# A GRU and an attention GRU on one core: a second copy of x on the state's quadrants, another order of the matmuls, halves for one product, and the second stage's sum on VectorE

## The reference, cut to what matters

```
xp = keys @ Wx + b_in                      # 64 -> 3*64, per step: xz, xr, xh
rec = h @ Wh + b_rec                       # rz, rr, rh
z = sigmoid(xz + rz);  r = sigmoid(xr + rr)
hh = relu(xh + r * rh)
h = z * h + (1 - z) * hh                   # 1024 steps, outputs kept
logit = sum_u(outs * (queries @ W_att.T)); attn = softmax over time
# second recurrence over outs, a = attn of the step
r = sigmoid(xr + h @ W_r);  c = relu(xc + r * (h @ W_c))
h = (1 - a) * h + a * c                    # 1024 steps, the last h is the output
```

## Time and profile before

| what | value |
|---|---|
| median of 3 runs | 4726.49 us |
| the profiled execution, its own time | 4727.85 us |
| its span (first to last instruction) | 4726.0 us |
| PE, PEld, DVE, ACT, POOL busy | 98%, 92%, 89%, 50%, 77% of the span |
| granted TensorE clock, mean share of full speed | 0.998 |
| DMA traffic over the span | 115 GB/s |

### The profile page before, as it was taken

One profiled execution on the slowest core, in us unless ns is written; L12 is line 12 of the kernel. 1 busy time (PEld: TensorE's weight loads), 2 busy tenths in 40 slices (PEclk: granted clock), 3 DMA queues, 4 the chain that ended last, 5 costly groups with the idle time before them and its releaser, 6 DMA issues.

```text
span 4726.0 us, 366111 instructions
## 1 busy us (share of the span) xinstructions
PE 4648.7 (98%) x131196; PEld 4341.8 (92%) x131196; DVE 4188.5 (89%) x28719; ACT 2353.4 (50%) x9363; POOL 3629.2 (77%) x8204
## 2 busy tenths in 40 slices
PE   8999999999999999999998999999999999999999
PEld 8999999999999999999997999999999999999998
DVE  8999999999999999999997888888888888888888
ACT  5555555555555555555553333333333333333333
POOL 6777777777777777777776888888888888888888
PEclk9999999999999999999999999999999999999999
DMA  3333333333333333333334554555555555555554
GB/s 103 107 107 114 110 107 113 110 107 111 113 107 111 113 107 108 115 108 107 115 116 119 124 122 118 124 123 119 122 124 119 121 124 120 120 124 120 119 124 108
DMA packets 169276, 544.15 MB, mean 115 GB/s; under 512 B 31644, under 2 KB 38060, under 8 KB 169260
## 3 DMA queue, kind: packets, MB, share of 16 engines
q1 hardware_dynamic: 169260, 543.93, 43.7%
HBM read 405.24 MB, written 138.56 MB: 115 GB/s over the span
## 4 chain that ended last, share of the span: by engine, by line
PE 98%; issue 1%; DMA 0%; DVE 0%; POOL 0%; SPq 0%; ACT 0%; POOLq 0%; ACTq 0%; DVEq 0%
PE r_bank_a L531 14%; PE r_bank_b L531 13%; PE c_bank_b L531 12%; PE c_bank_a L531 11%; PE logit_bank L583 6%; PE z_bank_a L537 6%; PE r_bank_a L537 5%; PE z_bank_b L537 5%; PE z_bank_a L531 5%; PE r_bank_b L537 5%; PE z_bank_b L531 4%; PE c_bank_b L537 3%; PE c_bank_a L537 3%; PE c_bank_a L543 1%; PE c_bank_b L543 1%
## 5 line engine op out<-in xcount | busy, mean ns | idle before, releaser
L295 POOL TENSOR_TENSOR kept<-z_gate,h 128x128 f32<-128x128 f32 x2048 | 931.8, 455 | 694.5 <-ACT z_gate L348 683.3
L316 POOL TENSOR_TENSOR a_kept<-attn_rest,state 128x128 f32<-128x128 f32 x2048 | 932.3, 455 | 276.7 <-POOL state L311 162.7
L311 POOL TENSOR_TENSOR state<-a_new,a_kept 128x128 f32<-128x128 f32 x2048 | 933.2, 456 | 122.0 <-DVE a_new L514 65.7
L285 POOL TENSOR_TENSOR prod<-h,qw 128x128 f32<-128x128 f32 x2050 | 933.6, 455 | 0.0
L537 PE MATMUL r_bank_a<-x,weights 64*64 64x128 f32 x8200 | 895.0, 288 | 14.0 <-ACT r_gate L377 7.9
L583 PE MATMUL logit_bank<-prod,row_sum 64*64 64x128 f32 x8208 | 895.3, 287 | 0.6 <-POOL prod L285 0.6
L537 PE MATMUL r_bank_b<-x,weights 64*64 64x128 f32 x8192 | 893.8, 288 | 0.0
L537 PE MATMUL z_bank_a<-x,weights 64*64 64x128 f32 x8200 | 876.4, 280 | 0.0
L537 PE MATMUL z_bank_b<-x,weights 64*64 64x128 f32 x8192 | 871.2, 278 | 0.2 <-DVE vec_bank L505 0.2
L444 DVE SCALAR_TENSOR_TENSOR vec_bank<-vec_bank,z_rest 128x64 f32<-128x64 f32 x4096 | 735.2, 225 | 0.3 <-issue 0.3
L455 DVE TENSOR_TENSOR h<-vec_bank,kept 128x64 f32<-128x64 f32 x4096 | 720.5, 218 | 0.3 <-issue 0.2
(11 more groups left out here) (119 smaller groups left out, 19328.3 us busy)
## 6 DMA issues: line engine op xcount, KB each, us to landing
x<-in_keys_t SPq DMA_DIRECT2D x512, 256.0 KB, 3.7
gru_outputs<-h SPq DMA_DIRECT2D x256, 512.0 KB, 3.3
x<-gru_outputs SPq DMA_DIRECT2D x512, 256.0 KB, 3.7
attn<-attention SPq DMA_DIRECT2D x512, 256.0 KB, 4.3
logits<-logit_rows SPq DMA_DIRECT2D x258, 8.0 KB
time_rows<-logits SPq DMA_DIRECT2D x2, 896.0 KB, 6.3
attention<-time_rows SPq DMA_DIRECT2D x2, 896.0 KB, 5.9
weights<-in_weight_columns SPq DMA_DIRECT2D x2, 176.0 KB, 3.7
```

The costliest lines, as they stand in the source:

```text
L285: nc.gpsimd.tensor_tensor(prod[:, (s - 1) % BODY, gcols(g)], h_at(s - 1)[:, gcols(g)], qw[:, gcols(g)], ALU.mult).then_inc(prod_ready[g], 1)
L295: nc.gpsimd.tensor_tensor(kept[:, g], z_gate[:, g], h_at(s - 1)[:, gcols(g)], ALU.mult).then_inc(kept_ready[g], 1)
L311: nc.gpsimd.tensor_tensor(state[:, (s - 1) % 2, gcols(g)], a_new[:, (s - 1) % 2, gcols(g)], a_kept[:, (s - 1) % 2, gcols(g)], ALU.add).the ...
L316: nc.gpsimd.tensor_tensor(a_kept[:, s % 2, gcols(g)], attn_rest[:, s % 2, gcols(g)], state[:, (s - 1) % 2, gcols(g)], ALU.mult).then_inc(a ...
```

## The change: what it does

1. **x twice.** A second tile `x_own` holds x with its halves in place. It is loaded by one DMA of 512 KB per chunk of 4 steps, beside the two of 256 KB for `x`. x's c term and both its biases run from it, in the straight quadrants (`own`, `own_bias`). The logit matmuls move to the crossed quadrants (the halves of the logit bank, and the rows stored from it, are swapped for it).
2. **Order of PE in the first stage.** A block is now: h's r term of g; x's r term of o; h's c term of g; h's z term of g; x's z term of o; x's c term of o; logit of g. The waits stand in three places: before the r term those for prod_ready of g, xr_summed of g, r_ready of o, h_ready of g (and x's loads); before the z term xz_summed; before x's z term z_rest and the second half of cand of o. h's c term and the DVE's `gru_cand` no longer wait for xh_summed, since the same quadrants run both in order.
3. **kept in halves.** POOL makes `kept` in two instructions of 64 columns, with a semaphore each; `gru_h` waits for its own half.
4. **Second stage.** `agru_gated`, `agru_cand` and `agru_new` are one instruction of 128 columns each instead of two of 64. `state` = a_new + a_kept moves from POOL to DVE (`agru_sum`), to stand between `agru_gated` of one group and its `agru_cand`, and sums the other group. On PE the wait for ar_ready of o moves ahead of a_new's r term, and the one for axr_summed ahead of a_kept's c term.

```diff
+            def load_x_own(k, b):
+                src = keys[k, b] if isinstance(k, int) else keys[bass.ds(k, 1), b].rearrange("a p s c -> (a p) s c")
+                sp.dma_start(x_own[:, b], src).then_inc(x_own_loaded[b], 16)
...
             for b in range(2):
                 load_x(keys, 0, b)
+                load_x_own(0, b)
             sp.wait_ge(split_done, 7)
...
-                        nc.gpsimd.tensor_tensor(kept[:, g], z_gate[:, g], h_at(s - 1)[:, gcols(g)],
-                                                ALU.mult).then_inc(kept_ready[g], 1)
+                        for part, c in PARTS:
+                            nc.gpsimd.tensor_tensor(kept[:, g, c], z_gate[:, g, c], h_at(s - 1)[:, gcols(g)][:, c],
+                                                    ALU.mult).then_inc(kept_ready[g][part], 1)
...
+            def agru_sum(done, s, g):
+                dve.wait_ge(akept_ready[g], done)
+                dve.wait_ge(anew_ready[g], done)
+                nc.vector.tensor_tensor(state[:, s % 2, gcols(g)], a_new[:, s % 2, gcols(g)],
+                                        a_kept[:, s % 2, gcols(g)], ALU.add).then_inc(s_ready[g], 1)
...
-                    for g in GROUPS:
-                        agru_gated(due, s, g)
-                        agru_cand(due, s, g)
-                        agru_new(due, pairs, s, g)
+                    agru_gated(due, s, 0)
+                    agru_sum(done, s - 1, 1)
+                    agru_cand(due, s, 0)
+                    agru_new(due, pairs, s, 0)
+                    agru_gated(due, s, 1)
+                    agru_sum(due, s, 0)
+                    agru_cand(due, s, 1)
+                    agru_new(due, pairs, s, 1)
...
             def gru_x_h(g, s):
-                last = from_x(inp_part(g), GX_H, x_at(s)[:, gcols(g)], True)
-                add_bias(inp_part(g), B_XH)
-                add_bias(hid_part(g), B_RH).then_inc(xh_summed[g], 1)
+                last = own(inp_part(g), GX_H, x_at(s, x_own)[:, gcols(g)], True, False)
+                own_bias(inp_part(g), B_XH)
+                own_bias(hid_part(g), B_RH).then_inc(xh_summed[g], 1)
                 return last
...
-                        alone()
-                        pe.wait_ge(h_ready[g], due)
-                        pe.wait_ge(xr_summed[g], due)
-                        own(r_bank[g][:, 0:GC], GH_R, hs, False, True).then_inc(r_summed[g], 1)
-
                         alone()
...
+                        pe.wait_ge(prod_ready[g], due)
+                        pe.wait_ge(xr_summed[g], due)
                         pe.wait_ge(r_ready[o], due_o)
+                        pe.wait_ge(h_ready[g], due)
+                        own(r_bank[g][:, 0:GC], GH_R, hs, False, True).then_inc(r_summed[g], 1)
                         gru_x_r(o, n)
+                        own(hid_part(g), GH_H, hs, False, True).then_inc(rh_summed[g], 1)
 
                         alone()
                         pe.wait_ge(xz_summed[g], due)
...
                         alone()
                         pe.wait_ge(zr_ready[o], due_o)
-                        gru_x_z(o, n)
-
-                        alone()
-                        pe.wait_ge(xh_summed[g], soon)
-                        own(hid_part(g), GH_H, hs, False, True).then_inc(rh_summed[g], 1)
-
-                        alone()
                         pe.wait_ge(cand_ready[o][1], due_o)
+                        last = gru_x_z(o, n)
...
                         last = gru_x_h(o, n)
                         if g == 0 and s % CHUNK == CHUNK - 1:
-                            last.then_inc(x_used, CHUNK)
-
-                        alone()
-                        pe.wait_ge(prod_ready[g], due)
...
+                            last.then_inc(x_own_used, CHUNK)
                         mm = logit(i, g, i == BODY - 1)
```

More of the change, by code:

```diff
@@ L77, in recurrent_attention_kernel @@
         x = sb("x", [P, 2, CHUNK, COLS])
+        x_own = sb("x_own", [P, 2, CHUNK, COLS])
         h = sb("h", [P, 2, CHUNK, COLS])
@@ L241, in _ @@
             sp.wait_ge(x_used, T)
-            sp.wait_ge(xh_summed[0], T + 2)
+            sp.wait_ge(xh_summed[0], T + 1)
+            sp.wait_ge(xz_summed[0], T + 1)
             for b in range(2):
@@ L278, in _ @@
             for g in GROUPS:
-                pool.sem_inc(kept_ready[g], 1)
+                for part, _ in PARTS:
+                    pool.sem_inc(kept_ready[g][part], 1)
                 pool.sem_inc(prod_ready[g], 1)
@@ L413, in _ @@
             for g in GROUPS:
[L414 removed]
+                for q in (*gated_ready[g], *cand_ready[g], *new_ready[g], agated_ready[g], acand_ready[g]):
                     dve.sem_inc(q, 1)
@@ L432, in gru_cand @@
                     dve.wait_ge(gated_ready[g][part], due)
-                    if part == 0:
-                        dve.wait_ge(xh_summed[g], due)
                     nc.vector.tensor_tensor(cand[:, c], inp_part(g)[:, c], gated[:, g, c],
@@ L494, in agru_gated @@
                 dve.wait_ge(rc_summed[g], due)
-                for part, c in PARTS:
-                    nc.vector.tensor_tensor(gated[:, g, c], c_bank[g][:, c], r_gate[:, g, c],
-                                            ALU.mult).then_inc(agated_ready[g][part], 1)
+                nc.vector.tensor_tensor(gated[:, g], hid_part(g), r_gate[:, g], ALU.mult).then_inc(agated_ready[g], 1)
             def agru_cand(due, s, g):
                 cand, _ = vec_parts(g)
-                for part, c in PARTS:
-                    dve.wait_ge(agated_ready[g][part], due)
-                    if part == 0:
-                        dve.wait_ge(axc_summed[g], due)
-                    nc.vector.tensor_tensor(cand[:, c], z_bank[g][:, c], gated[:, g, c],
-                                            ALU.add).then_inc(acand_ready[g][part], 1)
+                dve.wait_ge(agated_ready[g], due)
@@ L508, in agru_new @@
+                dve.wait_ge(axc_summed[g], due)
+                nc.vector.tensor_tensor(cand, z_bank[g][:, 0:GC], gated[:, g], ALU.add).then_inc(acand_ready[g], 1)
             def agru_new(due, pairs, s, g):
                 cand, _ = vec_parts(g)
-                for part, c in PARTS:
-                    dve.wait_ge(acand_ready[g][part], due)
-                    if part == 0 and g == 0 and s % CHUNK == 0:
-                        dve.wait_ge(a_loaded[s // CHUNK], pairs)
-                    last = nc.vector.scalar_tensor_tensor(a_new[:, s % 2, gcols(g)][:, c], cand[:, c], 0.0,
-                                                          attn_at(s)[:, gcols(g)][:, c], ALU.max, ALU.mult)
@@ L516, in agru_new @@
-                last.then_inc(anew_ready[g], 1)
+                dve.wait_ge(acand_ready[g], due)
+                if g == 0 and s % CHUNK == 0:
+                    dve.wait_ge(a_loaded[s // CHUNK], pairs)
+                nc.vector.scalar_tensor_tensor(a_new[:, s % 2, gcols(g)], cand, 0.0, attn_at(s)[:, gcols(g)],
+                                               ALU.max, ALU.mult).then_inc(anew_ready[g], 1)
+            def agru_sum(done, s, g):
[3 more added lines that the diff above has]
+                                        a_kept[:, s % 2, gcols(g)], ALU.add).then_inc(s_ready[g], 1)
@@ L527, in _ @@
+            agru_sum(T + 1, T - 1, 1)
         @block.tensor
@@ L545, in add_bias, with own_bias @@
                 return last
+            def own_bias(dst, part):
+                for half in range(HALVES):
+                    last = nc.tensor.matmul(dst[lanes(half)], bias_w[lanes(half), part], ones[lanes(half)],
+                                            start=False, stop=False, skip_group_check=True)
+                return last
             def alone():
                 pe.wait_ge(consts_ready, 3)
-            counts = [pe.alloc_register(f"pe_count_{i}") for i in range(4)]
+            counts = [pe.alloc_register(f"pe_count_{i}") for i in range(5)]
             def count(i, base, more):
@@ L559, in _ @@
             for g in GROUPS:
-                for q in (r_summed[g], rh_summed[g], z_summed[g], xh_summed[g], ar_summed[g], rc_summed[g], axc_summed[g]):
+                for q in (r_summed[g], rh_summed[g], z_summed[g], ar_summed[g], rc_summed[g], axc_summed[g]):
                     pe.sem_inc(q, 1)
@@ L582, in logit @@
                 for half in range(HALVES):
-                    mm = nc.tensor.matmul(logit_bank[lanes(half), gcols(g)],
+                    mm = nc.tensor.matmul(logit_bank[lanes(1 - half), gcols(g)],
                                           row_sum[lanes(half), BODY - 1 - i:BODY - 1 - i + U],
@@ L649, in _ @@
             pe.wait_ge(id_ready, 1)
-            pe.wait_ge(xh_summed[0], T + 2)
+            pe.wait_ge(xh_summed[0], T + 1)
+            pe.wait_ge(xz_summed[0], T + 1)
             for g in GROUPS:
```

72 lines of the change are left out of this document (36 added, 36 removed).

## The result

The changed kernel takes 5123.76 us (median of 4 runs, 5109.32 to 5136.55), the kernel before 4727.04 (4 runs): a ratio of 1.084 (95% interval 1.081 to 1.087). The forecast was 4842, from 4695 to 4950. The sign was right and the size was not: 397 us are to be explained, where 116 were forecast.

A forecast was written before the change was run, and what follows sets the result against it. The c loop (2.32 us a step) was taken to bound the first stage, a loop through cand (2.12) the second. 4726.0 + 51 + 61 + 3.5 = 4841.5 span, giving a 4842 us median; range 4695 to 4950.

The forecast's parts named there:

- Start: Kernel start: x_own's first chunks queue ahead of the bias loads, +3.5 us (3 to 5); added steady-loop traffic costs nothing.
- Waits gathered: First stage, PE: r now waits for its group's prod_ready, closing a loop of 2.27 us plus the cost of halving.
- product loop: First stage: r, z, z_gate, kept, prod, r sets the step at 2.37 us instead of 2.32, +51 us.
- Halving: POOL's kept in two instructions: adds 0.10 us to the product loop, bounds 0 and 0.20.
- kept loop: First stage, through kept and h's second half: r could start again at 2.24 us, under the product loop's 2.37.
- rival 3: First stage: prod isn't last, DVE's 2.19 us bounds the step, 133 us gained, 4658 us; chance 0.13.
- The second stage: DVE's sum between gated and cand makes cand end 0.065 us later a step, +61 us (0 to +92).
- PE's waits there change places [...] nothing: Second stage, PE: the moved waits leave the order of matmuls as it was and cost nothing.
- That a wait stands for several semaphores may add some hundredths: First stage, waits gathered before r: several semaphores may add some hundredths of a us, left to the upper end.
- Rival 5: Second stage: DVE and POOL collide on their shared interface, cand up to 0.25 us late, about 5100 us; chance 0.03.

The follow-up runs named there:

- e1: Changed kernel, but SP stores a body's logits after its first chunk's work instead of its second: 4935.78 us, 1.044.
- e21: e1 with only the wait for the logits' copy put back in front of the logit matmul: 4865.42 us, 1.029.
- e6: Changed kernel with logits stored early, waits for prod and logits' copy back at the logit matmuls, and the second stage of before: 4717.45 us, 0.998.
- e8: Kernel before with the change's second-stage full width and moved PE waits, but the state sum left on POOL: 4775.04 us, 1.010.
- e14: e8 with PE's wait for axr_summed put back behind a_kept's c term: 4710.99 us, 0.997.
- e22: e9 with the logits store put ahead of the second chunk's loads: 4733.53 us, 1.001.
- e9: Kernel before, also loading the second copy of x, which nobody reads: 4906.39 us, 1.037.
- e4: Kernel before with only the second-stage parts of the change: 4790.96 us, 1.014.
- e15: e4, sum on VectorE, with PE's wait for axr_summed put back behind a_kept's c term: 4794.27 us, 1.014.
- e10: e6 with the waits gathered before r parted: h's r term keeps h_ready and xr_summed, x's r term takes r_ready and the loads: 4717.14 us, 0.998.
- e16: e10 with the wait for h_ready declared ahead of that for xr_summed: 4675.30 us, 0.989.

## Why the prediction was wrong

Bodies of the first stage, in turn, times 128, and the rest:

```
late store of the logits   21.75 -> 20.27  (after -> e1)   190 us
copy's wait ahead of r     20.27 -> 19.71  (e1 -> e21)      72
product's wait ahead of r  19.71 -> 19.09  (e21 -> e6)      79
all else in that stage     19.09 -> 19.19  (e6, before)    -13
second stage               2286 for 2219                    67
start                      16.05 for 13.35                   3
sum                                                        398   (measured 397)
```

The third and the fourth row are sharp to some 15 us only: e6 has the second stage of before, and such a change alone moved the bodies of the first by up to 0.12 (e8, e14).

- **The step that failed** is the last sentence under *Start*: "In the steady loop a third more is moved [...] nothing". It weighed bandwidth and stopped there. (By its own figures, 110 to 165 GB/s, it is a half more; 164 was measured in e22.) Bandwidth was free (e22); the place in the queue wasn't (e9). The prediction never asked which transfer stands behind the new ones and who waits for it. SP issues every transfer of the loop, and in the code the logits come last. That is 190 us, with no place in any rival; 38 of them come through the clock, as told at the end.
- **A wait left out.** *Waits gathered* lists r's waits for prod_ready, r_ready and xr_summed, and not the `logits_copied` one that the change moves in the same lines. The description of the change leaves it out too. At the logit it stood behind a block of work; ahead of r it holds up the block: 72 us.
- **The product loop** was right: steady 2.375 for a forecast of 2.37, r 0.09 after prod, prod later than h. Two sizes in it were off and cancelled: z_gate came 0.05 earlier than forecast and prod 0.04 later. Halving costs 0.14 (0.60 from the first half's start to the second's end, where the whole took 0.455), not 0.10. The estimate by the Trainium skill (GPSIMD Engine Reference, § 3.1 Elementwise — side-by-side cycle accounting), 0.14, was the better one. Over the run the loop costs 79 - 13 = 66 us where 51 were forecast. Of the 15 more, 10 are the step itself, which grew by 0.060 (2.315 to 2.375) and not by 0.05. The rest is what a body's ends leave: from before to e21 the first step grows by 0.28 and the seventh by 0.15, and the last shrinks by 0.22.
- **That the kept loop would be short**, 2.24, was wrong: 2.337 (e6). z_gate's link was shorter, but kept's pair and the h halves came to 0.93 for 0.84, and h to r took 0.15. It was hidden in the change, and is why rival 3 had no gain to reach: even without prod's wait the change's own order is worth 13 us, which is no more than first stages differ by without an edit.
- **The second stage**, +61 forecast, +67 measured, `cand` 0.41 after `gated` for 0.40. The size and its place are right (e4, e15); the prediction's own 0.065 a step, not rounded to 0.06, gives 67. "PE's waits there change places [...] nothing" is wrong taken by itself: without the sum, that edit costs as much (e8, e14). Two faults of one size stood behind each other, and undoing only one of them would have made it look free.
- **"That a wait stands for several semaphores may add some hundredths"** was right as a worry (0.045) and wrong in its cause: their order does it, not their number (e10, e16). It was no part of the change's own steady step, which the product set.
- **Start**: +2.7 for +3.5 (3 to 5). Rival 5, a collision of VectorE and POOL, didn't come: `agru_sum` takes 0.28.

## What to carry to other kernels

Before a transfer is added, list what the same queue carries behind it, who waits for each, however small, and how much time it has in hand: bandwidth to spare says nothing of an 8 KB store. A wait moved to the head of an in-order block is to be priced for the step where it is latest, once per body, not for the steady step. Where two waits stand in front of one matmul, try declaring the late one first and look at the gap in the trace. When an edit is undone and nothing moves, undo its neighbour as well before calling it free.

## What the runs showed of the hardware

- Two waits in front of one matmul: with the late one (h) declared last, r starts 0.146 us after h, declared first 0.100 (e10, e16), and 42 us over the run. Why the order matters, no run shows.
- The bias matmul's record in e8 ends at 3502.85, and its semaphore's update stands in the trace at 3503.04, 0.19 later. The matmul that it held starts at 3503.17, 0.135 after that, which is also what r takes after h's update where h is declared last. The Trainium skill (Perfetto Trace Analysis, Tensor Engine Instruction) says that these ends are estimated and not observed, and the trace agrees: x's c term would have let the matmul go at 3503.10, so by the records the wait was met 0.25 before it was wanted, and by the semaphore 0.06.
- POOL's product of 64 columns takes 320 ns, of 128 columns 455: 2.1 ns a column and 185 ns fixed.
- TensorE's clock fell after some of the longer stalls of the changed kernel: in 30 of 126 bodies, with 4.3 to 5.1 us between two r terms, though in 18 others with a stall as long it didn't. The windows of one, in which r of step two came 4.44 us after the last:

```profile
266.00:268.50 2.50, 1.72 (x58) 1.44 (x52) 2.48 (x18) 1.24 (x6) 1.90 (x7) 1.00 0.79 306
268.50:271.00 2.50, 1.24 (x29) 1.27 (x33) 0.39 (x4) 0.66 (x2) 0.20 (x1) 0.82 0.00 0
271.00:273.40 2.40, 2.40 (x53) 2.40 (x52) 1.69 (x11) 1.12 (x5) 1.05 (x4) 0.50 0.00 0
273.40:276.00 2.60, 2.52 (x86) 2.37 (x82) 2.42 (x16) 1.46 (x7) 2.04 (x7) 0.98 0.12 30
```

  0.50 is the lower of its two levels, 1.2 GHz, and the step after the stall took 3.56 for 2.375. In those 30 bodies the four steps after the stall take 1.26 us more together than the median ones, which is 38 us of the 190. In e1 one stretch of the stage has the lower clock.
- Bodies of the first stage took 19.08 us for 19.19 in kernels that differ from the one before in the second stage only (e8, e14; 19.13 in e4 and e15): 15 us, more than the 0.2% by which a change was to be told. Why, these runs don't show.
